# Where the edge-weight rests of a convolutional LSTM are subtracted: VectorE or GpSimd

## The reference

```python
feat = jnp.concatenate([jnp.broadcast_to(x_i, x_j.shape), x_j - x_i], axis=-1)
h = jnp.einsum('bnkc,oc->bnko', feat, ew) + eb
h = jax.nn.gelu(h * es + et, approximate=False)
h = jnp.max(h, axis=2)
...
return y + tmp          # y = affine(conv1x1(h, fc2)), tmp = the input
```

```python
def step(carry, xr):
    h, c = carry
    inp = jnp.concatenate([xr, h], axis=1)
    gates = lax.conv_general_dilated(inp, w_mid, (1,), 'SAME', dimension_numbers=dn) + b[None, :, None]
    i, f, g, o = jnp.split(gates, 4, axis=1)
    c2 = jax.nn.sigmoid(f) * c + jax.nn.sigmoid(i) * jnp.tanh(g)
    h2 = jax.nn.sigmoid(o) * jnp.tanh(c2)
    return ((h2, c2), h2)
```

## Time and profile before

| what | us |
|---|---|
| median of 3 runs | 661.46 |
| lowest and highest run | 658.25, 665.33 |
| the profiled execution, its own time | 663.54 |
| span of its trace, first to last instruction | 661.7 |

### The profile page before, as it was taken

One profiled execution on the slowest core, in us unless ns is written; L12 is line 12 of the kernel. 1 busy time (PEld: TensorE's weight loads), 2 busy tenths in 40 slices (PEclk: granted clock), 3 DMA queues, 4 the chain that ended last, 5 costly groups with the idle time before them and its releaser, 6 DMA issues.

```text
span 661.7 us, 12838 instructions
## 1 busy us (share of the span) xinstructions
PE 581.0 (88%) x3404; PEld 340.8 (51%) x3404; DVE 508.2 (77%) x970; ACT 432.7 (65%) x639; POOL 253.6 (38%) x298
## 2 busy tenths in 40 slices
PE   5956699999999999949979989999999999988970
PEld 1212455565555555625545656666665655545530
DVE  2688699999999999956998656666667577655665
ACT  3723278888888888937886645566555556644555
POOL 2740023333334433313865534444444344324310
PEclk9968599999999999978998989999999999979985
DMA  9937656656656566585531122112212222285616
GB/s 226 270 111 210 184 134 133 140 138 136 145 138 141 139 141 144 137 163 125 132 73 33 40 64 50 48 48 52 49 33 58 73 80 66 67 179 111 140 54 190
DMA packets 101605, 76.00 MB, mean 115 GB/s; under 512 B 52610, under 2 KB 84868, under 8 KB 101236
## 3 DMA queue, kind: packets, MB, share of 16 engines
q1 hardware_dynamic: 100804, 71.94, 44.8%
q10 hardware_dynamic: 768, 3.67, 2.2%
HBM read 49.08 MB, written 22.15 MB: 108 GB/s over the span
## 4 chain that ended last, share of the span: by engine, by line
PE 46%; DVE 21%; issue 10%; DMA 8%; ACT 7%; SPq 6%; DVEq 1%; POOL 1%; ACTq 0%; POOLq 0%
PE pz L700 9%; PE pz L610 7%; PE pz L679 7%; DVE onehot L1183 5%; PE pz L694 5%; PE p_edge L700 4%; ACT gel L819 4%; PE p_edge L679 4%; DVE hmax L1198 3%; DVE idx L1174 3%; DMA y_d<-y 3%; PE p_edge L694 2%; PE p_keys L558 2%; DVE val L1166 2%; DMA y_hl<-y_d 2%
## 5 line engine op out<-in xcount | busy, mean ns | idle before, releaser
L1198 DVE TENSOR_REDUCE hmax<-gel 96x128 f32<-96x1024 f32 x128 | 151.7, 1204 | 19.8 <-ACT gel L819 19.7
L819 ACT ACTIVATE gel<-pz 96x1024 f32<-96x1024 f32 x128 | 131.0, 1024 | 47.2 <-PE pz L610 42.7
L1087 POOL CAST ht<-h 48x512 fp32r<-48x512 f32 x62 | 37.6, 607 | 157.3 <-DVE h L1304 156.7
L700 PE MATMUL pz<-ht,w_xh 128*112 128x512 f32 x258 | 74.8, 427 | 6.5 <-DMA ht<-xh 6.5
L1089 POOL TENSOR_TENSOR ht<-h,ht 48x512 fp32r<-48x512 f32 x62 | 73.5, 1186 | 5.0
L679 PE MATMUL pz<-xh,w_xh 128*112 128x512 f32 (+1 forms) x258 | 70.0, 408 | 0.0
L610 PE MATMUL pz<-onehot,ab_hi 64*96 64x512 f32 x256 | 62.0, 481 | 3.3 <-ACT gel L819 2.6
L700 PEld LDWEIGHTS pz<-ht,w_xh 128*112 128x112 f32 x258 | 43.4, 181 | 34.1 <-issue 19.9
L881 ACT ACTIVATE pz<-c 48x512 f32<-48x512 f32 x43 | 25.7, 599 | 48.3 <-DVE c L1297 48.3
L679 PEld LDWEIGHTS pz<-xh,w_xh 128*112 128x112 f32 x258 | 46.6, 181 | 17.0 <-issue 0.4
L1304 DVE SCALAR_TENSOR_TENSOR h<-tgo,pz 48x512 f32<-48x512 f32 x43 | 29.7, 690 | 30.3 <-ACT pz L881 30.3
(11 more groups left out here) (145 smaller groups left out, 1243.4 us busy)
## 6 DMA issues: line engine op xcount, KB each, us to landing
ib<-idx_d SPq DMA_DIRECT2D x64, 256.0 KB, 4.1
y_d<-y SPq DMA_DIRECT2D x32, 192.0 KB, 3.3
y_hl<-y_d SPq DMA_DIRECT2D x32, 192.0 KB, 4.0
hist_d<-h SPq DMA_DIRECT2D x62, 96.0 KB, 1.9
hp<-hist_d SPq DMA_DIRECT2D x30, 192.0 KB, 2.6
kr<-xn_d SPq DMA_DIRECT2D x32, 98.0 KB
xn_d<-x_in SPq DMA_DIRECT2D x32, 96.0 KB, 2.2
kl<-xn_d SPq DMA_DIRECT2D x32, 96.0 KB
```

Source lines behind the costliest of these rows:

```text
L700: mm = pe.matmul(gate_banks(k, d)[m][0:TOP, :], w_xh[:, 1, d, m, t], moving(ht, slice(0, P), t), start=False, stop=(t == TAPS - 1))
L819: act.activation(gel[:, t % 2], pz[0:O, 2 * (t % 2):2 * (t % 2) + 2, :], ACT.Gelu) \
L1087: pool.tensor_copy(h_slots(ht, 0, d), columns(h2[0:C, d])).then_inc(S["h_top"], 1)
L1198: dve.tensor_reduce(dst, gel[:, t % 2].rearrange("p w (r c k) -> p w r c k", r=WS, k=KN), AX_X, ALU.max).then_inc(S["maxed"], 1)
```

## The change

The subtraction that makes `w_e` is taken out of VectorE's turn 1 of group 31 and given to GpSimd, ahead of `h_parts(0, 0)`. There GpSimd waits for `wl_heads` at 3 (the rounded head is there) and for `self_maxed` at 32 (the last self maximum of VectorE is done), subtracts, and waits for its own result before it goes on. TensorE's wait ahead of step 1 and SyncE's wait ahead of the loads that reuse the memory of `wl_raw` and `wl_head` go to the new semaphore `w_e_ready`. The operation, its operands and its 128 x 1344 values stay the same. ScalarE's instructions stay as they are.

```diff
-            sp.wait_ge(S["wl_split"], 3)
+            sp.wait_ge(S["w_e_ready"], 1)
...
             fc2(GROUPS - 1, 1, GROUPS // 2 - 1)
-            pe.wait_ge(S["wl_split"], 3)
+            pe.wait_ge(S["w_e_ready"], 1)
             step(1, 1, 0, 1)
...
             x1_low_first(GROUPS - 2, 0, GROUPS // 2 - 1)
             pool.wait_ge(S["x1_half"], GROUPS - 1)
+            pool.wait_ge(S["wl_heads"], 3)
+            pool.wait_ge(S["self_maxed"], GROUPS)
+            passed(pool, "pool_passed")
+            pool.tensor_tensor(w_e[:], wl_raw[:, 2], wl_head[:, 0].bitcast(F32), ALU.subtract).then_inc(S["w_e_ready"], 1)
+            pool.wait_ge(S["w_e_ready"], 1)
             h_parts(0, 0)
...
                 elif g == GROUPS - 2:
                     dve.wait_ge(S["wl_split"], 1)
                     head(2)
-                else:
-                    dve.wait_ge(S["wl_heads"], 3)
-                    dve.tensor_tensor(w_e[:], wl_raw[:, 2], wl_head[:, 0].bitcast(F32), ALU.subtract) \
-                        .then_inc(S["wl_split"], 1)
```

More of the change, by code:

```diff
@@ L192, in build @@
             x1_stored0 x1_stored1 sp_passed dve_passed pool_passed
-            wl_loaded wl_scaled wl_heads wl_split rests_set rests_here gates tanh_if tanh_go cells cells_kept cell_parts tanh_c
+            wl_loaded wl_scaled wl_heads wl_split w_e_ready rests_set rests_here gates tanh_if tanh_go cells cells_kept cell_parts tanh_c
             x_twin00 x_twin01 x_twin10 x_twin11 x_third0 x_third1
```

## The result

The changed kernel takes 656.94 us (median of 22 runs, 652.76 to 665.88) against 662.07 us for the kernel before in as many runs: ratio 0.9935, 95% interval 0.9915 to 0.9955. That is 4.3 us faster (3.0 to 5.6). The ratio and its interval leave out one far slower run of either kernel (665.88 and 2831.39 us), and aren't the quotient of the two medians, which is 0.9923 or 5.1 us. The median lies inside of the forecast's range (655.4 to 663.4 us), which would have held a kernel without any gain too, and the gain is under the line of 1%. A second comparison gave 0.9935 again (0.9906 to 0.9965). The forecast was 2.9 us. So the direction and the places were right, and 1.4 us came from somewhere else.

The account below looks back on a forecast made before the run. The subtraction on VectorE was taken to be on the path at the junction, with TensorE the bound later. From the median of 661.46 us, 1.5 us of path and 1.4 us of clock gave 658.6 us, range 655.4 to 663.4.

Parts of the forecast that it names:

- The subtraction off VectorE's path: VectorE, last group: self maximum, first cell and TensorE's step 1 come 1.5 us earlier, bounds 1.4 to 1.77 us.
- The wait for the last GELU: VectorE, ahead of the third maximum: 0.2 to 0.3 us of the 1.77 us freed go to this new wait.
- The subtraction on GpSimd: GpSimd, ahead of the cast of h(0,0): takes 2.8 us, at most 5.0, and costs nothing.
- The cover: GpSimd's time until the cast of h(0,0): 3.5 us, of which 2.95 us are needed and 0.55 us spare.
- The first fall of the clock: TensorE, step 1: without the idle stretch its clock stays at 1.00, worth 1.4 us, between 0 and 1.55.
- The step that failed: Scan behind step 1: all moves forward whole, idle stretch and low clock at step 3's third part staying as they are.
- The DMA of that third part: Step 3's third part, issued at 380.24: hangs on h(1,1) by waits and would be issued at about 377.3.
- That GpSimd would become the bound: Rival: GpSimd and VectorE hold each other off in the first cell, 662.2 us; chance 0.08.
- That the gain is lost later: Rival: step 3's third part or the scan's end is held by something that did not move, 661.5 us; chance 0.08.
- That the clock falls all the same: Rival: TensorE's clock falls at step 1 anyway, so only the first term is left, 660.0 us; chance 0.22.

Follow-up runs that it names:

- e1_before: The kernel before, no edit, run once more for a second trace; 663.89 us in a single run.
- e4_double: Changed kernel with the subtraction done twice on GpSimd, TensorE and SyncE waiting for the second; ratio to before 1.0024 (0.9993 to 1.0055).
- e7_late_before: Kernel before with SyncE doing steps 2 and 3 ahead of its last-split wait and four constant loads; ratio to before 0.9940 (0.9907 to 0.9974).
- e10_shorter: Kernel before with SyncE's load of comb_sb moved behind step 13; ratio to before 1.0002 (0.9970 to 1.0034).
- e5_early: Changed kernel without GpSimd's wait for the last self maximum ahead of the subtraction; ratio to before 0.9933 (0.9899 to 0.9966).
- e9_longer: Changed kernel with one of SyncE's four loads of constants cut in two; ratio to before 0.9966 (0.9936 to 0.9997).
- e2_after: The changed kernel, no further edit, run once more for a second trace; ratio to before 0.9935 (0.9906 to 0.9965).
- e11_after: The changed kernel, no further edit, run for one more trace; 655.78 us in a single run.
- e8: Changed kernel with SyncE doing steps 2 and 3 ahead of its last-split wait and four constant loads; ratio to before 0.9918 (0.9887 to 0.9948).
- e3: Kernel before with six more matmuls, result never read, in TensorE's wait ahead of step 1; ratio to before 0.9974 (0.9943 to 1.0006).
- e6: Subtraction kept on VectorE but put behind its first h(0,0), ahead of direction 1's cell; ratio to before 0.9991 (0.9961 to 1.0021).

## Why the prediction was right, and what it missed

**The subtraction off VectorE's path: right, and a little more than said.** 1.5 us were forecast; the self maximum ends 1.67 us earlier in two traces of three (7.65 to 5.98) and h(0,0) by the same; in the one whose GELUs ran late they come 1.26 and 0.78 us earlier. The wait for the last GELU that I took 0.2 to 0.3 us for took 0.02 us in the shown trace, since there it ended at 360.06 us, just as the second maximum did. At the third part, e1_before against the changed kernel, both without the first fall, is 31.60 to 29.66: 1.94 us.

**The subtraction on GpSimd: right, sized low.** 2.8 us forecast, 3.12 measured, so 2.3 ns a column beyond 512 instead of 1.94. The estimate of 2.95 us from the Trainium skill, "GPSIMD Engine Reference", section 3.1, was nearer. The cover was 3.5 us as forecast, of which 0.39 us were left idle where 0.55 were expected; e4_double shows what lies past it.

**The first fall of the clock: the mechanism was right, its size an average that I didn't take.** 1.4 us forecast, 1.46 measured where it happens (33.06 to 31.60). It happened in two of three traces of before and in none of the changed kernel, which over these three makes some 1.0 us. e7_late_before and e10_shorter have before's order up to there and had it too, in e10 at a price of 2.6 us; by all five the average is nearer to 1.3.

**The step that failed** is the one that put the rest of the scan at no change: "so it moves forward whole; its idle stretch and its low clock stay as they are". It moved forward whole, but the idle stretch shrank from 1.83 or 1.89 to 1.55 us, and the low clock behind it, there in three of three traces of before, was gone in all four traces that have the change with its single subtraction and the old order of SyncE (the three of the table and e5_early). That is worth some 1.25 us and 0.3 more. e9_longer brought it back by lengthening that stretch alone, and e7_late_before and e10_shorter took it away without the change, in one trace each. The DMA of that third part, which the prediction moved by 2.9 us, is issued 3.4 us sooner after the common point (31.09 to 27.68): 1.7 for the path, 1.46 for the first fall and 0.3 for a cast of GpSimd (below).

So the length of the stretch has a part in it. It doesn't decide alone. Later in the scan, e2_after had idle stretches of 2.48 and 2.04 us and e11_after of 2.48 and 2.27 us without a fall, while the changed kernel's first trace fell behind one of 1.50 us. TensorE's timeline and the busy time by stretch behind it, in e2_after:

```profile
601.74 1.66 PE L700 MATMUL pz<-ht,w_xh 128*112 128x512 f32 x6 [2.04 <-DMA ht<-xh]
```

```profile
602.00:607.00 5.00, 4.99 (x23) 3.23 (x22) 2.91 (x5) 2.54 (x5) 0.69 (x1) 1.00 0.83 195
```

The same two views in the trace of the changed kernel that was shown first:

```profile
613.02 1.82 PE L700 MATMUL pz<-ht,w_xh 128*112 128x512 f32 x5 [1.50 <-DMA ht<-xh]
```

```profile
614.00:617.00 3.00, 3.00 (x8) 2.13 (x8) 2.27 (x4) 1.80 (x3) 0.49 (x1) 0.50 0.84 224
```

What else the grant answers to, when the stretch comes or what TensorE did ahead of it, no run varied by itself.

The sum over the traces: 1.7 for the path, 0.3 for the shorter idling, 1.0 and 1.25 for the clock, 4.2 us, or 3.9 with e11_after's late start counted in. The mean of h(25,0) over three traces each is 223.11 and 219.28 us, 3.8 apart, against 4.3 us (3.0 to 5.6) of the measured ratio. The forecast's 2.9 us had the path too low by 0.2 and the average price of the first fall too high by up to 0.4, and left out 0.3 and 1.25. So in part its errors cancel.

**Why the second wait is shorter by 0.3 us** is seen, but its root is not explained. The last h of step 1 ended at 24.31, 22.86 and 24.31 us in the traces of before and its cast on GpSimd started 0.47 or 0.48 us behind; with the change it starts 0.17 us behind. All kernels with the added instruction on GpSimd have 0.17 (changed kernel, e4, e5, e8, e9) and all without have 0.47 or 0.48 (before, e3, e6, e7, e10). The last split and SyncE's loads follow this cast in order, so its 0.30 us are the 0.3 us of the wait. But they did not simply vanish: in the changed kernel's three traces, e8 and e9, the cast ahead of it, that of h(1,0), starts 0.47 us behind its `h` instead of 0.17, where nothing on the path waits for it; e4 and e5 have the delay at neither. It looks as if something held GpSimd up for 0.30 us at one place of its instruction stream, which added instructions move. What it is stays open. No run changed it alone.

**The rivals.** That GpSimd would become the bound is refuted for one subtraction and shown for two. That the gain is lost later is refuted: h(25,0) keeps it, and so does the measured time. That the clock falls all the same was the case in no trace of the changed kernel, at the place for which it was asked.

Left open is the last stretch: from h(25,0) to the last h, the traces of before take 66.0 to 66.6 us, the changed kernel's 66.5, 63.6 and 62.6. Its two longest idle stretches, ended by DMAs (4.5 to 5.0 us in all in either kernel), are followed by falls of the clock in some traces and not in others. Over all fourteen traces this stretch takes 62.6 to 66.5 us with the subtraction on GpSimd and 63.7 to 66.7 us without. Whether the change has a share in it, the traces are too few to say. This scatter of 4 us is as large as the gain, so that the 3.8 us at h(25,0) lie near the measured 4.3 isn't a proof of the sum.

## What to carry to other kernels

A step of little work can be worth more than its duration when it stands ahead of a serial chain: price it by what TensorE idles for behind it, and by what the clock does after that, at every idle stretch downstream and not only at the first. When work goes to another engine, its price is the cover that it finds there; compute it from the wait that this engine shows, look for two-input operations of VectorE beside it, and double the work once to see where the cover ends. When a trace shows a fall of the clock, take a second trace of the same kernel before you sum with it, and read the price of each fall from a pair of traces with and without it: here one cost 1.46 us, another 1.25 and a long one 2.6.

## What the runs showed of the hardware that I had not expected

- The clock fell to 0.50 behind all ten idle stretches of TensorE of 1.83 us or more at these two places (1.83, 1.83, 1.85, 1.89, 1.89 and 2.08 ahead of the third part; 1.92, 1.96, 2.64 and 3.53 ahead of step 1), behind two of six of 1.54 to 1.59 us, and behind none of seven of 0.28 to 1.26 us. These are counts of this kernel's traces, in which much else about the stretches is alike, and they don't hold later in the scan, where 2.04 to 2.48 us of idling passed four times without a fall.
- At these two places a fall lasted some 3 us, and some 7 us in e10_shorter. It cost 1.46 us (first place) and some 1.25 us (second) in the first form, and 2.6 us in the other.
- A cast on GpSimd of 0.60 us took 1.90 us beside a two-input subtraction of VectorE, while one on GpSimd of 3.12 us took no time from VectorE's cell operations, which kept their 0.69 and 0.70 us. Where it began 0.31 us into VectorE's self maximum (e5_early) it took 3.34 us, and the self maximum kept its 0.69.
- With the subtraction added to GpSimd's stream, its fourth cast (of h(1,1)) started 0.30 us sooner behind its `h`, and in five of seven such traces the third cast 0.30 us later.
